# Two token mixers: loops over sequences written out, and the delta rule's second chunk and transposes issued ahead of the second pair's half products

## The chip, the cores and the metric

The kernel runs on one core of one Trainium2 chip. The metric is the device time of the whole program in microseconds (us). A time quoted for a kernel is the median of its runs; a profile is one execution, and its times inside the trace are counted from its first instruction.

## What is computed

Sixteen sequences of 512 tokens with 256 channels go through four layers, each followed by a residual sum and a layer norm, all in float32:

```
x = norm(x + linear_attention(x))     # first mixer: gated, 8 heads
x = norm(x + top2_experts(x))         # 8 experts, capacity limit
x = norm(x + delta_rule(x))           # second mixer: gated delta rule, 4 heads
x = norm(x + composed_mlp(x))         # weights mixed from 32 of 64 primitives
```

The recurrence of the second mixer, for each head, with a state S of 64 by 128:

```
S = S * exp(g_t)
delta = (v_t - k_t S) * b_t
S = S + k_t (x) delta
o_t = q_t S
```

It is worked in chunks of 128 tokens, four to a sequence. A chunk needs the inverse of a unit triangular 128 by 128 matrix for each head. The diagonal blocks of 16 by 16 are inverted on their own, and three rounds of products (levels 4, 5 and 6) merge them to the full inverse.

## The kernel before

There are five parts one after the other: linear attention (the first mixer), routing, the experts, the delta rule (the second mixer) and the closing MLP. In both mixers every engine runs the same order written by hand, one body (`body`) or period (`period`) for each sequence, and engines meet at counting semaphores. The flags of a period say which stages it holds: `front` (projection, convolution and rates of sequence b+1), `here` (the recurrence's first half of sequence b), `past` (second half and output of b-1), `ln` (norms of b+2) and `end` (the last norm of b-2). The first and last periods are written out. The twelve between them, sequences 2 to 13, were a hardware loop of six rounds with two bodies in each:

```
with eng.Fori(0, (B - 4) // 2) as i:
    for u in range(2):
        period(i * 2 + 2 + u, u, here=True, front=True, ln=True, past=True, end=True)
```

Inside the loop the sequence number is a register, and so are the semaphore counts worked out from it.

In the delta rule the order of a period came from 16 slots, eight for each pair of chunks. Slots 5 to 7 and 13 to 15 hold the three levels of a pair. TensorE (PE), for a level and a chunk: `first_half` transposes T into bank UT (L2359) and multiplies (L2363); ScalarE (ACT) copies both results out in `half_level` (U at L2108, Y at L2110); `second_half` multiplies again (L2375, L2377); VectorE (DVE) puts the result into T in `merge` (L1831, or L1826 at level 6, where it is U). UT is one bank, so the next chunk's `first_half` waits for the copy of U.

The diagonal blocks leave and come back by DMA. `key_products` (PE, L2344) gives the products, `key_decays` (DVE, L1809) scales them, `send_blocks` (SyncE's queue) writes them out, GpSimd (POOL) inverts them, and `return_blocks` brings them into T once ACT's `restart` has cleared T. `first_half` of level 4 waits for that landing (`T<-blocks_in`). The factors come from `scan` (DVE, L1800), which `key_decays` needs too.

`chunk(t, part)` is the recurrence itself: part 0 reads the state (PE L2294, L2298; DVE's R at L1843), part 1 is `dl` (PE L2304, copied out by ACT at L2097), part 2 updates state and output (PE L2311, L2315; DVE L1849, L1852). `channels` is PE's twelve transposes of each half of keys and queries of the next sequence (L2275), which ACT's `channel` copies out (L2041). `conv` is DVE's three-step convolution (L1729); it stands between ACT's `tap` (L2007) before it and `conv_silu` (L2012) after it. `reach` (PE, L2332) needs the last of `rates` on DVE (L1771). `norm2` is DVE's L1709 and L1711. In a row, `<-` behind a wait names what ended it.

Of the kernel before, what the change touches and what calls it, by code (L numbers as in the profile page):

```python
# [12 lines left out]
ALU = mybir.AluOpType  # L13
# [4 lines left out]
B, L, D = 16, 512, 256  # L18
NTOK = B * L
DT = D // P  # L20
TT = L // P
# [546 lines left out]
def linear_attention(nc, x_rows, xT_rows, conv_w, wq, wkg, wv, wg, bg, wout, aug_bal, w_gate, x1_rows, logits_out):  # L568

    with ExitStack() as ctx:  # L570
# [87 lines left out]
        with nc.Block() as block:  # L658
# [83 lines left out]
            def _(dve):  # L742
# [190 lines left out]
            def _(act):  # L933
# [105 lines left out]
                with act.Fori(0, (B - 4) // 2) as i:  # L1039
                    for u in range(2):  # L1040
                        body(i * 2 + 2 + u, u, i * 2 + 1 + u, True, i + 2)
# [3 lines left out]
            def _(pe):  # L1045
# [174 lines left out]
                with pe.Fori(0, (B - 4) // 2) as i:  # L1220
                    for u in range(2):
                        body(i * 2 + 2 + u, u, i * 2 + 1 + u, True, i + 2)
# [7 lines left out]

CHUNK_AT = {0: (2, 0), 1: (2, 1), 2: (2, 2), 3: (3, 0), 4: (3, 1), 5: (3, 2),
            9: (0, 0), 10: (0, 1), 11: (0, 2), 12: (1, 0), 13: (1, 1), 14: (1, 2)}
# [121 lines left out]
def delta_rule(nc, x1_rows, slots_out, get_at, weight, ln1_g, ln1_b, rms_w, wq, wk, wv, conv_q, conv_k, conv_v, wa, dt_bias, a_log, wb, wg,  # L1354
               o_norm, wo, ln2_g, ln2_b, w2, b2, x2_rows, hT_rows, blocks_out, blocks_in, x3_wide, fc1, fc2, out_rows):

    with ExitStack() as ctx:
# [115 lines left out]
        def loop(eng, period):  # L1473

            starts(period)
            with eng.Fori(0, (B - 4) // 2) as i:
                for u in range(2):
                    period(i * 2 + 2 + u, u, here=True, front=True, ln=True, past=True, end=True)
            ends(period)

        with nc.Block() as block:
            @block.sync
            def _(sp):
# [81 lines left out]
                loop(sp, period)  # L1565
# [3 lines left out]
            def _(pool):  # L1569
# [88 lines left out]
                loop(pool, period)  # L1658
# [3 lines left out]
            def _(dve):  # L1662
# [128 lines left out]
                def scan(pair, b):  # L1791
                    wait, done = waiter(dve, b)
                    for t in (2 * pair, 2 * pair + 1):
                        i = t % 2
                        wait("aB", t + 1)
                        if t >= 2:
                            wait("kd", t - 1)
                        elif later(b, 0):
                            dve.wait_ge(s["kd"], (b - 1) * TT + t + 3)
                        done("DT", t + 1, v.tensor_tensor_scan(flat(DT_[i][:]), bank[CHUNK[i]][:], flat(id4[:]), 0.0, ALU.mult, ALU.add))  # L1800
# [102 lines left out]
                def period(b, u, here=False, front=False, ln=False, past=False, end=False):  # L1903
                    w = 1 - u
                    for slot in range(2 * (LEVELS + 1)):
                        pair, lv = slot // (LEVELS + 1), slot % (LEVELS + 1) - 1
                        t, part = CHUNK_AT.get(slot, (None, None))
                        if here and lv < 0:
                            key_decays(pair, b)
                        if t is not None and t >= 2 and past:  # L1910
                            chunk(t, part, b - 1, w)
                        if here and lv < 0:
                            query_decays(pair, b)
                        if front and slot == 8:
                            conv(6, b + 1)
                            conv(7, b + 1)
                        if slot == 10 and front:
                            rates(1, b + 1)
                            keys_beta(b + 1)
                        if slot == 11 and past:  # L1920
                            residual(0, b - 1)
                        if t is not None and t < 2 and here:
                            chunk(t, part, b, u)
                        if front and 1 <= slot <= 6:
                            conv(slot - 1, b + 1)
                        if slot == 7 and front:
                            lengths(b + 1)
# [643 lines left out]
```

## Time and profile before

| | us |
|---|---|
| median of 3 runs | 4533.56 |
| lowest and highest run | 4521.59, 4539.57 |
| the profiled execution | 4549.05 |
| its span in the trace | 4547.4 |
| first mixer | 0 to 866 |
| routing, experts | 866 to 2068 |
| delta rule | 2068 to 4072 |
| closing MLP | 4072 to 4547 |

The span is that from the first to the last instruction; 1.65 us of the execution lie outside it. The profiled execution is 15.5 us above the median of the runs. The share of busy time differs much between the parts, so each is read by itself.

### The profile page before, as it was taken

How to read it: one execution, taken by the hardware profiler on the slowest of the kernel's cores; microseconds unless marked ns; L12 is line 12 of the kernel's file. 1: busy time of each engine (PE TensorE's matmuls, PEld its weight loads, DVE VectorE, ACT ScalarE, POOL GpSimd, SP SyncE). 2: the span in 40 equal slices, each digit the busy share in tenths (PEclk: the TensorE clock that was granted, in tenths of full speed). 3: DMA queues.
4: the chain of work that ended last, by engine and by line, in shares of the span. 5: the costliest groups of instructions: out<-in, count | busy, mean ns of one | idle time of the engine just before them, and what ended most of it. 6: DMA issues, size and time to landing. Idle time of an engine off the chain costs nothing.

```text
span 4547.4 us, 72522 instructions
## 1 busy us (share of the span) xinstructions
PE 3962.4 (87%) x23860; PEld 3063.0 (67%) x23860; DVE 2468.9 (54%) x5456; ACT 1990.0 (44%) x4069; POOL 1100.5 (24%) x1686
## 2 busy tenths in 40 slices
PE   6888788598999999994798888888888888879998
PEld 3555555377888888883576666676676677756666
DVE  6888888452222222224577777777777777431111
ACT  5656555111212222122466666666666666432221
POOL 0111111101222222212334444443334343200000
PEclk8888889699999999997799999999999999889999
DMA  1010010254555555552111111111111110011111
GB/s 34 29 42 29 28 40 22 64 147 167 184 183 183 183 183 183 184 181 82 38 35 42 43 43 43 43 43 43 43 42 43 43 43 24 19 58 55 55 55 51
DMA packets 220956, 346.98 MB, mean 76 GB/s; under 512 B 99972, under 2 KB 171908, under 8 KB 202500
## 3 DMA queue, kind: packets, MB, share of 16 engines
q1 hardware_dynamic: 196932, 272.74, 18.9%
q0 software_dynamic: 23760, 71.07, 5.0%
q8 instruction: 123, 2.02, 0.2%
q14 instruction: 141, 1.16, 0.1%
HBM read 276.61 MB, written 68.16 MB: 76 GB/s over the span
## 4 chain that ended last, share of the span: by engine, by line
PE 23%; POOL 8%; issue 8%; DVE 8%; ACT 4%; DMA 2%; SPq 2%; POOLq 0%; DVEq 0%; ACTq 0%
PE gdr_bank L1320 5%; PE gdr_bank L1311 5%; DVE gdr_y L1729 3%; POOL gdr_vblk L1628 2%; PE gdr_bank L2363 2%; POOL gdr_tblk L1626 2%; PE gdr_bank L2375 1%; PE gdr_bank L2240 1%; PE gdr_bank L2359 1%; SPq L1519 1%; POOL gdr_ssq L1616 1%; PE gdr_bank L2408 1%; POOL gdr_orr L1616 1%; POOL gdr_got L1582 1%; POOL gdr_vblk L1623 1%
## 5 line engine op out<-in xcount | busy, mean ns | idle before, releaser
L525 ACT ACTIVATE moe_rel<-moe_fc 128x512 f32<-128x512 f32 x284 | 169.6, 597 | 798.5 <-PE moe_fc L490 798.5
L490 PE MATMUL moe_fc<-moe_xT,moe_win 128*128 128x256 f32 x2272 | 503.8, 380 | 1.5 <-issue 0.8
L501 PE MATMUL moe_o<-moe_wout,moe_hT 128*128 128x256 f32 x2272 | 502.0, 379 | 0.0
L490 PEld LDWEIGHTS moe_fc<-moe_xT,moe_win 128*128 128x128 f32 x2272 | 432.7, 191 | 61.2 <-issue 2.1
L501 PEld LDWEIGHTS moe_o<-moe_wout,moe_hT 128*128 128x128 f32 x2272 | 426.3, 190 | 55.1
L549 DVE TENSOR_TENSOR moe_hT<-moe_rel 128x512 f32<-128x512 f32 x284 | 196.6, 692 | 361.3 <-ACT moe_rel L525 361.3
L1729 DVE SCALAR_TENSOR_TENSOR gdr_y<-gdr_bank,gdr_cw,gdr_y 128x511 f32<-128x511 f32 (+2 forms) x384 | 287.5, 749 | 51.1 <-ACT gdr_y L2007 28.9
L2240 PE MATMUL gdr_bank<-gdr_hT,gdr_wqkv 128*128 128x512 f32 x512 | 263.6, 645 | 31.9 <-ACT gdr_qk L2022 26.8
L558 DVE COPY moe_osb<-moe_o 128x512 f32<-128x512 f32 x71 | 49.1, 692 | 424.9 <-PE moe_o L501 424.9
L2359 PE MATMUL gdr_bank<-gdr_ident,gdr_T 128*128 128x128 f32 x768 | 136.0, 306 | 109.7 <-DMA gdr_T<-blocks_in 95.0
L1311 PE MATMUL gdr_bank<-gdr_hT,gdr_wqkv 128*128 128x512 f32 x512 | 225.4, 599 | 3.5 <-ACT gdr_hT L1329 3.5
L1344 DVE TENSOR_TENSOR gdr_kb<-gdr_bank,gdr_x 128x512 f32<-128x512 f32 x32 | 20.6, 686 | 366.4 <-PE gdr_bank L1320 366.4
L2359 PEld LDWEIGHTS gdr_bank<-gdr_ident,gdr_T 128*128 128x128 f32 x768 | 101.2, 158 | 153.0 <-DMA gdr_T<-blocks_in 73.8
L2363 PE MATMUL gdr_bank<-gdr_T,gdr_nAT 128*128 128x64 f32 (+1 forms) x1536 | 197.6, 278 | 0.0
L2363 PEld LDWEIGHTS gdr_bank<-gdr_T,gdr_nAT 128*128 128x128 f32 (+1 forms) x1536 | 187.3, 198 | 10.9 <-issue 10.9
L2108 ACT COPY gdr_U<-gdr_bank 128x512 f32<-128x512 f32 x192 | 112.4, 585 | 184.4 <-PE gdr_bank L2359 173.9
L2240 PEld LDWEIGHTS gdr_bank<-gdr_hT,gdr_wqkv 128*128 128x128 f32 x512 | 92.7, 199 | 145.5 <-issue 74.4
L1311 PEld LDWEIGHTS gdr_bank<-gdr_hT,gdr_wqkv 128*128 128x128 f32 x512 | 98.3, 192 | 121.2 <-issue 120.4
L446 POOL COPY moe_ix<-slot_token 128x2 uint32 (+1 forms) x71 | 13.0, 183 | 659.9 <-DMA slots_out<-moe_osb 471.8
L1616 POOL TENSOR_TENSOR gdr_rstd<-gdr_var,gdr_mhalf 128x4 f32<-128x4 f32 x64 | 70.9, 1107 | 391.5 <-DVE gdr_var L91 263.5
L450 POOL DMA_INDIRECT moe_xin<-token_rows,moe_ix x142 | 137.3, 967 | 82.8 <-POOL moe_ix L446 58.2
L1333 ACT ACTIVATE gdr_sq<-gdr_bank 128x512 f32<-128x512 f32 x64 | 38.2, 597 | 257.2 <-PE gdr_bank L1311 257.2
(391 smaller groups left out, 8843.1 us busy)
## 6 DMA issues: line engine op xcount, KB each, us to landing
moe_win<-in_moe_w SPq DMA_DIRECT2D x71, 1024.0 KB, 7.9
moe_wout<-in_moe_w SPq DMA_DIRECT2D x71, 1024.0 KB, 5.1
slots_out<-moe_osb POOLq DMA_DIRECT2D x71, 256.0 KB, 7.4
gdr_fz<-mixed_rows SPq DMA_DIRECT2D x18, 512.0 KB, 3.8
gla_xp<-in_xT_rows SPq DMA_DIRECT2D x16, 512.0 KB, 4.7
gla_xres<-in_x_rows SPq DMA_DIRECT2D x16, 512.0 KB, 3.9
token_rows<-gla_x POOLq DMA_DIRECT2D x16, 512.0 KB, 3.4
rt_W<-in_fc_b SPq DMA_DIRECT2D x32, 256.0 KB, 3.4
```

Source lines behind the costliest of these rows:

```text
L450: nc.gpsimd.indirect_dma_start(xin[t][:], None, x_rows, bass.IndirectOffsetOnAxis(ap=ix[:, t:t + 1], axis=0)).then_inc(x_in, 16)
L490: ins = nc.tensor.matmul(fc_ps[j][:, m % 2, :], win[u][:, c, m * P:(m + 1) * P], xT[:, c, :], start=(c == 0), stop=(c == DT - 1))
L501: ins = nc.tensor.matmul(o_ps[u][:, t, :], hT[u][:, k, t * P:(t + 1) * P], wout[u][:, k, :], start=(k == 0), stop=(k == FT - 1))
L525: nc.scalar.activation(rel[:, j, :, :], fc_ps[j][:], ACT.Relu).then_inc(relu_done, 1)
L549: nc.vector.tensor_tensor(hT[u][:, 2 * j:2 * j + 2, :], rel[:, j, :, :], rel[:, j, :, :], ALU.mult).then_inc(h_ready, 1)
L1311: ins = nc.tensor.matmul(fc_ps[m % 4][:], win[:, c, m * P:(m + 1) * P], xT[:, c, :], start=(c == 0), stop=(c == DT - 1))
L1320: ins = nc.tensor.matmul(o_ps[t // 2][:, (t % 2) * D:(t % 2 + 1) * D], hT[k][:, t * P:(t + 1) * P], wout[:, k, :], start=(k == 0), stop=(k ...
L1616: nc.gpsimd.tensor_tensor(out, src, mhalf[:, 0:width], ALU.pow).then_inc(s[name], 1)
L1729: ins = stt(y[:, n % 4, d:L], bank[FRONT[n % 2]][:, 0:L - d], cw[:, n, 3 - d:4 - d], y[:, n % 4, d:L], ALU.mult, ALU.add)
L2240: ins = mm(bank[FRONT[n % 2]][:], wqkv[:, c, n * P:(n + 1) * P], hT[:, c, :], start=(c == 0), stop=(c == DT - 1))
L2359: ins = tp(bank[UT][:, h * P:(h + 1) * P], T[:, i, h, :], ident[:])
L2363: ins = mm(bank[YZ[i]][rows_of(lv), h * HP:(h + 1) * HP].rearrange("p (m n) -> p m n", n=half), nAT[:, i, h, rows_of(lv)], first, start=Tr ...
```

## The change

Both mixers' loops are written out, so that sequence numbers and semaphore counts are constants and no engine branches in them. In the delta rule the table of slots gives way to one written list for each engine. On PE, the second chunk's `dl` and all transposes of the next sequence's second half stand ahead of the second pair's first half product, and `reach` behind part 2 of chunk 0. On DVE, level 4's merges of the first pair stand ahead of `conv(4)`, level 6's merges of the first pair between the two scans, both residuals behind part 2 of chunk 0, `norm2` behind part 0 of chunk 1, and both scans of the next sequence ahead of the bias. On ACT, `restart(1)` stands behind the rates, the copies of `channel` around chunk 1's parts, and `lengths_u`, `keep_keys` and the squares of chunk 0 behind the copies of level 4 or 5. No instruction of the engines' work is added or taken out; SyncE's and GpSimd's lists keep their order.

```
-                with dve.Fori(0, (B - 4) // 2) as i:
-                    for u in range(2):
-                        body(i * 2 + 2 + u, u, i * 2 + 1 + u, True, i + 2)
+                for b in range(2, B - 2):
+                    body(b, b % 2, b - 1, True, b // 2 + 1)
...
-        def loop(eng, period):
+        def loop(period):
...
-            with eng.Fori(0, (B - 4) // 2) as i:
-                for u in range(2):
-                    period(i * 2 + 2 + u, u, here=True, front=True, ln=True, past=True, end=True)
+            for b in range(2, B - 2):
+                period(b, b % 2, here=True, front=True, ln=True, past=True, end=True)
```

VectorE (the written list; conditions on the flags are as before):

```
-                def scan(pair, b):
+                def scan(t, b):
...
+                        chunk(3, 2, b - 1, w)
+                    if here:
+                        merge(4, 0, b)
+                        merge(4, 1, b)
+                    if front:
+                        conv(4, b + 1)
...
+                        scan(2, b)
+                        merge(6, 0, b)
+                        merge(6, 1, b)
+                        scan(3, b)
+                        key_decays(1, b)
+                        query_decays(1, b)
...
+                        rates(1, b + 1)
+                        keys_beta(b + 1)
+                    if here:
+                        chunk(0, 2, b, u)
+                    if past:
+                        residual(0, b - 1)
+                        residual(1, b - 1)
+                    if here:
+                        chunk(1, 0, b, u)
+                    if ln:
+                        norm2(b + 2)
+                    if here:
+                        merge(4, 2, b)
+                        merge(4, 3, b)
```

ScalarE:

```
+                        rates(0, b + 1, w)
+                    if here:
+                        decay_keys(2, b)
+                        decay_keys(3, b)
+                        chunk(0, 1, b, u)
+                    if front:
+                        rates(1, b + 1, w)
+                    if here:
+                        restart(1, b)
+                    if front and here:
+                        act.wait_ge(s["ks"], b * TT + 2)
+                    if front:
+                        channel(0, 0, b + 1, w)
+                        channel(0, 1, b + 1, w)
+                        channel(0, 2, b + 1, w)
+                        channel(1, 0, b + 1, w)
+                    if here:
+                        chunk(1, 0, b, u)
+                        chunk(1, 1, b, u)
+                    if front:
+                        channel(1, 1, b + 1, w)
+                        channel(1, 2, b + 1, w)
+                    if here:
+                        half_level(4, 2, b)
+                        half_level(4, 3, b)
+                    if ln:
+                        lengths_u(b + 2)
```

TensorE:

```
+                    if here:
+                        chunk(0, 1, b, u)
+                        chunk(0, 2, b, u)
...
+                        reach(b + 1)
+                        channels(0, (0, 1), b + 1)
+                    if here:
+                        chunk(1, 0, b, u)
+                    if front:
+                        channels(0, (2,), b + 1)
+                        channels(1, (0,), b + 1)
+                    if here:
+                        chunk(1, 1, b, u)
+                    if front:
+                        channels(1, (1, 2), b + 1)
+                    if here and past:
+                        pe.wait_ge(s["xe"], b * 2)
+                    if here:
+                        first_half(4, 2, b)
+                        first_half(4, 3, b)
+                        second_half(4, 2, b)
+                        second_half(4, 3, b)
+                        first_half(5, 2, b)
+                        chunk(1, 2, b, u)
```

## Rows read from the trace of the kernel before

**Rows 1.** Windows, the delta rule's part: length, busy of each engine, PEclk, DMA share, GB/s.

```profile
2068.00:4072.00 2004.00, 1669.86 (x10696) 1314.17 (x10696) 1364.97 (x3156) 1175.38 (x2789) 727.47 (x1279) 0.91 0.15 42
```

**Rows 2.** Windows of the first mixer's bodies: one written out, two in the loop.

```profile
101.90:149.50 47.60, 40.23 (x377) 26.93 (x377) 43.61 (x85) 30.35 (x45) 7.42 (x3) 0.89 0.11 34
...
543.00:593.40 50.40, 40.57 (x378) 27.17 (x378) 42.22 (x83) 29.57 (x44) 8.02 (x4) 0.86 0.10 32
593.40:641.80 48.40, 40.27 (x379) 26.95 (x378) 42.28 (x83) 29.58 (x44) 8.02 (x4) 0.89 0.10 33
```

**Rows 3.** Waits of VectorE in the first loop: total us, times, longest.

```profile
DVE gla_mu L843 <- issue: 15.3, 5, 3.3
```

**Rows 4.** Windows of the delta rule: periods 8, 9 and 13, the twelve in the loop.

```profile
3096.10:3213.50 117.40, 105.36 (x669) 83.45 (x668) 85.91 (x198) 73.25 (x174) 44.68 (x79) 0.91 0.14 37
3213.50:3328.40 114.90, 99.28 (x671) 78.11 (x670) 85.23 (x198) 73.26 (x174) 45.91 (x79) 0.97 0.17 46
...
3677.70:3790.50 112.80, 98.97 (x669) 78.16 (x668) 85.21 (x198) 73.25 (x174) 36.58 (x67) 0.97 0.12 34
...
2402.20:3790.50 1388.30, 1214.85 (x8017) 960.83 (x8016) 1026.27 (x2376) 879.04 (x2088) 538.75 (x936) 0.95 0.15 41
```

**Rows 5.** Waits of TensorE in the delta rule's loop.

```profile
PE gdr_bank L2359 <- DMA gdr_T<-blocks_in: 61.0, 24, 4.1
...
PE gdr_bank L2294 <- issue: 9.8, 5, 2.6
```

**Rows 6.** Timeline of TensorE, period 9, second half: start, length, instructions, idle before.

```profile
3286.81 0.37 PE L2332 MATMUL gdr_bank<-gdr_sp,gdr_upto 128*128 128x16 f32 x2 [1.43 <-DVE gdr_sp L1771]
...
3297.78 1.11 PE L2359 MATMUL gdr_bank<-gdr_ident,gdr_T 128*128 128x128 f32 x4 [3.99 <-DMA gdr_T<-blocks_in]
...
3300.28 2.02 PE L2304 MATMUL gdr_bank<-gdr_R,gdr_U 128*128 128x128 f32 x8
3302.10 1.06 PE L2359 MATMUL gdr_bank<-gdr_ident,gdr_T 128*128 128x128 f32 x4
...
3305.99 1.04 PE L2275 MATMUL gdr_bank<-gdr_ident,gdr_qk 128*128 128x128 f32 x8
...
3307.77 0.60 PE L2359 MATMUL gdr_bank<-gdr_ident,gdr_T 128*128 128x128 f32 x4
```

**Rows 7.** Timeline of TensorE, period 9, first half.

```profile
3247.73 1.90 PE L2375 MATMUL gdr_bank<-gdr_Y,gdr_U 128*128 128x64 f32 x16
...
3251.39 0.66 PE L2359 MATMUL gdr_bank<-gdr_ident,gdr_T 128*128 128x128 f32 x4
...
3252.99 0.65 PE L2359 MATMUL gdr_bank<-gdr_ident,gdr_T 128*128 128x128 f32 x4
...
3266.37 0.50 PE L2344 MATMUL gdr_bank<-gdr_XT 64*128 64x128 f32 x4 [1.56 <-DVE gdr_U L1826]
```

**Rows 8.** Timeline of VectorE, period 9.

```profile
3248.40 2.31 DVE L1729 SCALAR_TENSOR_TENSOR gdr_y<-gdr_bank,gdr_cw,gdr_y 128x511 f32<-128x511 f32 x3
...
3251.49 0.44 DVE L1831 COPY_PREDICATED gdr_T<-gdr_level,gdr_bank 128x256 f32<-128x256 int32 x1 [0.15 <-DVE gdr_T L1831]
...
3264.55 1.23 DVE L1800 TENSOR_TENSOR_SCAN gdr_DT<-gdr_bank,gdr_id 128x512 f32<-128x512 f32 x1 [0.19 <-DVE gdr_DT L1800]
3265.90 0.95 DVE L1826 COPY gdr_U<-gdr_bank 64x256 f32<-64x256 f32 x2
...
3293.70 1.67 DVE L1709 SCALAR_TENSOR_TENSOR gdr_fz<-gdr_xn,gdr_rstd,gdr_g 128x256 f32<-128x256 f32 x4
...
3296.66 1.13 DVE L1843 SCALAR_TENSOR_TENSOR gdr_R<-gdr_bank,gdr_gbn,gdr_v 128x128 f32<-128x128 f32 x4
```

**Rows 9.** Timeline of ScalarE, period 9, between the two levels.

```profile
3250.81 0.63 ACT L2012 ACTIVATE gdr_y<-gdr_y 128x512 f32<-128x512 f32 x1 [2.24 <-DVE gdr_y L1729]
...
3252.35 0.58 ACT L2108 COPY gdr_U<-gdr_bank 128x512 f32<-128x512 f32 x1
```

**Rows 10.** DMA queues in the delta rule's loop: packets, MB, share of 16 engines.

```profile
q8 instruction: 72, 1.18, 0.4%
```

More of the change, by code:

```diff
@@ L1657, in period @@
                         constants()
-                loop(pool, period)
+                loop(period)
                 fc_gpsimd(pool)
@@ L1980, in _ @@
+                    if past:
+                        bias(1, b - 1)
+                loop(period)
                 fc_vector(dve)
@@ L2216, in _ @@
-                loop(act, period)
+                    if past:
+                        chunk(2, 0, b - 1, w)
+                    if front:
+                        tap(0, b + 1)
+                    if end:
+                        gelu(b - 2)
+                    if front:
+                        tap(1, b + 1)
+                    if past:
+                        chunk(2, 1, b - 1, w)
+                        gate(0, b - 1)
+                    if front:
+                        conv_silu(0, b + 1)
@@ new lines, in period @@
+                    if here:
+                        decay_keys(0, b)
+                        restart(0, b)
+                    if front:
+                        spread_out(0, b + 1)
+                    if past:
+                        gate(1, b - 1)
+                    if front:
+                        conv_silu(1, b + 1)
+                        tap(2, b + 1)
+                    if here:
+                        decay_keys(1, b)
+                    if past:
+                        chunk(3, 0, b - 1, w)
@@ L2503, in _ @@
-                loop(pe, period)
+                    if past and here:
+                        pe.wait_ge(s["DT"], b * TT + 2)
+                    if past:
+                        chunk(2, 0, b - 1, w)
+                    if here and past:
+                        pe.wait_ge(s["Uf"], b * TT)
+                    if here and end:
+                        pe.wait_ge(s["yb"], (b - 1) * 2)
+                    if here:
+                        key_products(0, b, u)
+                    if front:
+                        project(0, b + 1)
+                        project(1, b + 1)
@@ new lines, in period @@
+                    if past:
+                        for c in range(1, DH):
+                            mix_out(c, b - 1)
+                    if here:
+                        chunk(0, 1, b, u)
+                        chunk(0, 2, b, u)
+                    if front and not later(b, -1):
+                        pe.wait_ge(ready, 1)
+                        pe.wait_ge(aprep, 3)
+                    if front:
+                        reach(b + 1)
+                        channels(0, (0, 1), b + 1)
@@ new lines, in period @@
+                    if past:
+                        dense(0, b - 1)
+                    if here:
+                        first_half(6, 3, b)
+                        second_half(6, 2, b)
+                        second_half(6, 3, b)
+                    if ln and front:
+                        pe.wait_ge(s["qkT"], (b + 2) * 6)
+                    if ln:
+                        turn_h(b + 2)
+                    if past:
+                        dense(1, b - 1)
+                loop(period)
```

542 lines of the change are left out of this document (271 added, 271 removed).

## The prediction, made before the run

> **What bounds the kernel now.** I read the windows by part first. The delta rule is the longest of the parts touched: TensorE (PE) is busy for 1669.86 of its 2004 us, VectorE (DVE) for 1364.97 [rows 1]. In the first mixer it is the other way round: a body of the loop takes 48.40 us, in which DVE is busy for 42.28 and PE for 40.27 [rows 2]. So the first mixer is read on DVE and the delta rule on PE.
>
> Next come the waits. In the first loop DVE stands still five times, 15.3 us in all, with nothing that the profile shows to wait for, each time at the first instruction behind the loop's turn [rows 3]. In the delta rule's loop PE does the same five times, 9.8 us in all [rows 5]. Six rounds make five turns, and neither view has such a wait on these lines anywhere else. PE's largest wait is for the diagonal blocks: 61.0 us over 24 landings, two in each of the twelve periods [rows 5].
>
> The timeline of period 9 then shows the order around that landing. PE waits 3.99 us for the second pair's blocks; only after it come chunk 1's `dl`, from 3300.28, and the second half's transposes, from 3305.99 [rows 6].
>
> **The change part by part.** The sum is made against the profiled execution's 4549.05 us and then carried over to the median, 4533.56, which is 15.5 us lower.
>
> *First mixer, the turn of the loop.* A body with the turn in it takes 50.40 us, one without 48.40 [rows 2]: 2.0 us, five times, -10. The gaps themselves add up to 15.3 [rows 3], which is the other bound; the difference of the bodies is what the span pays, so I take 10.
>
> *First mixer, counts as constants.* The body written out before the loop takes 47.60 us against 48.40, though its DVE has more to do, 43.61 against 42.28 [rows 2]. Twelve bodies would give 9.6; but that body also stands at the start, where PE and the first loads are differently placed. I take half, -4.8, with 0 and 9.6 as ends.
>
> *Delta rule, the turn and the counts.* The gaps are 9.8 us [rows 5], and PE is the bound there, so that is the lower end. Period 13, which a written-out period follows, takes 112.80; the twelve took 1388.30, and twelve of 112.80 would be 1353.6, so the upper end is 34.7 [rows 4]. Period 9 less one mean gap of 1.96 is 112.9, like period 13. So the odd periods go there; whether the even ones do isn't shown. I take 20: the gaps, and two fifths of the rest.
>
> A rule of the Trainium skill speaks against both of these terms. The rows show 3.1 us for a gap of DVE and 2.0 for one of PE [rows 3, 5]. The Trainium skill's page "Advanced Engine Details and Errata", section Control Flow Timing, gives a compare-and-branch about 108 ns. By that figure ten turns cost about 1 us, an estimate, where the gaps cost 20, and the sum below would be about 19 smaller. I go by the rows.
>
> *Delta rule, second half.* From 3300.28 to 3302.10 and from 3305.99 to 3307.77 PE works on what now goes ahead of the landing: 1.82 + 1.78 = 3.60 us a period [rows 6]. It can go there only if its inputs are ready. R of chunk 1 is made at 3296.66, behind `norm2`, which starts at 3293.70; the new order puts R first, so it is there some 2.9 us earlier [rows 8], about 3294.9. With ACT's copies between the transposes I find PE through with the moved work at about 3297.0, ahead of the landing at 3297.78 [rows 6]. What hides it is that wait. `reach` and its 1.43 us of waiting [rows 6] also move, behind chunk 0's part 2, and so does `restart(1)`: costed at nothing, because both lie ahead of the same landing; without that cover 1.4 more would be gained.
>
> Two things are taken off. `key_decays` of the second pair now stands behind a scan of 1.23 us [rows 8] that used to be done before the copies; DVE waits for PE there, and I put 0.5 on the landing. And `first_half`, `first_half`, `second_half`, `second_half`, `first_half` now follow each other with nothing between: a copy of U is 0.58 [rows 9], a merge 0.44 [rows 8], each mostly under the other chunk's products; I put 0.9 for the waits. That leaves 2.2 us, for the 15 periods that have both stages: -33. Ends: 0, if the blocks come later by all that was won; and 5.7, if PE's lower clock in that stretch goes too. Four transposes took 1.11 us behind the landing and 0.66 at 3251.39 [rows 6, 7]; of the 9.99 us from 3297.78 to 3307.77, 6.39 aren't moved, and at 0.66 for 1.11 they would take 3.8, so 3.60 + 2.6 - 0.5.
>
> *Delta rule, first half.* Here the change adds a wait. `conv(4)` starts at 3248.40 [rows 8]; now the two merges of level 4 stand ahead of it, and the second can't start before PE's `second_half` ends at 3247.73 + 1.90 = 3249.63 [rows 7]. With a merge of 0.44 behind that, `conv(4)` starts near 3250.3, 1.9 later. Behind it on ACT are `conv_silu`, `tap` and only then level 5's copy of U, which starts 1.64 us after the convolution's end [rows 8, 9]. PE's next transposes, at 3252.99 [rows 7], need that copy at once: they go to 3254.9. What the earlier merge gives PE is next to nothing here, as its first transposes of level 5 began at 3251.39, as soon as `project` was through [rows 7]. In return the copies of level 6 go between the scans: PE's wait of 1.56 at 3266.37 was for these, which came at 3265.90 behind a second scan begun at 3264.55 [rows 7, 8]; up to 1.35 is saved. The one wait moves into the other: 1.9 less 1.35 and what is left of the 1.56. I take 0, with -1.35 and +1.9 a period as ends, -20 and +29.
>
> *Sum.* -10 - 4.8 - 20 - 33 + 0 = -68. Against the profiled execution 4481; against the median 4465, which I predict. All ends on the good side would give 15.3 + 9.6 + 34.7 + 86 + 20 = 166 less, all on the bad one 10 + 9.8 less and 29 more, about +9.
>
> **Rivals.** Times are from the median.
>
> 1. *The late convolution isn't made up.* DVE waits for ACT's squares before the scans, so the 1.35 is not found: +29, 4494. For it: PE's copy of U was just in time, with no slack [rows 7, 9]. Against: the 1.56 of idle time is there to swallow it. Chance 0.18.
>
> 2. *The lower clock behind the landing goes too,* because the wait before it shrinks from 4 us to about 1. Half of the 2.6 and the 0.9 of new waits come back: 2.2 more a period, -33, 4432. Against it: PE still waits for copies between the moved pieces. Chance 0.11.
>
> 3. *Slower: the new wait costs PE its clock.* Periods 8 and 9 run the same instructions, yet PE is busy for 105.36 us in the one, at a mean granted clock of 0.91, and for 99.28 in the other at 0.97 [rows 4]: 6.1 us. If the 1.9 us of waiting at level 5 brings that to twelve more periods, it is +73, and with rival 1's 29 the time is 4567. It decides from about eleven such periods on. Against it: period 9 has its waits without it. Chance 0.07.
>
> 4. *Written-out code runs dry.* If each of 24 written-out bodies had one gap of 2.0, in place of ten gaps now, 28 would be lost and 20 not won: 4513. Against: inside the loop instructions are already streamed, 72 packets of 1.18 MB on one queue [rows 10], and the gaps are at turns alone [rows 3, 5]. Chance 0.05.
>
> 5. *The gap isn't the turn's* and stays at the head of a body: 19.8 less is won, 4485. This is what the page's figure for a branch would give. Chance 0.05.
>
> The forecast has 0.54.
>
> **How the numbers follow.** About 0.5% is what a measurement of this kernel can tell from no change: 4511 to 4556. The forecast, rivals 1, 2 and 5 end below that, but for some of their spread; rival 4 on its edge; rival 3 above. That gives faster 0.85, same 0.09, slower 0.06. The range reaches from beyond rival 2, with the first half's gain, 4405, to 4515, which takes in rivals 1, 5 and 4; rival 3 and the far ends stay out.
>
> **What would show it.** After the change neither "issue" wait is left on L843's and L2294's successors. A body of the first mixer takes 47.6 to 48.4 throughout. PE's wait for the blocks falls from 4 us to about 1 for the second pair and stays as it is for the first. A new wait of about 1.9 us stands before the second chunk's transposes of level 5, and the wait of the second pair's key products is gone or small. A period takes about 110 to 111. I am wrong if the blocks land later than their chain of today, if `restart(1)` becomes what their return waits for, or if periods at a clock of 0.91 become the rule.

## The result, and the profile after

| | us |
|---|---|
| before, median of 4 runs beside it | 4529.94 |
| after, median of 4 runs | 4478.48 (4467.55 to 4483.57) |
| ratio, 95% interval | 0.9876 (0.9844 to 0.9907) |
| predicted | 4465, range 4405 to 4515 |
| profiled execution after, its span | 4473.65, 4472.0 |

The kernel became 56 us faster by the ratio (0.0124 of 4534); the sum had said 68. The runs below show that the total came near by luck: the delta rule's loop and its second half gave more than their terms, and its first half, put at nothing, cost 40 to 54 us.

First the windows of the changed kernel: a body of the first mixer, then periods 11 and 12, then the fourteen periods 1 to 14 in one window, each with length, busy time of PE, PEld, DVE, ACT and POOL, PEclk, DMA share and GB/s.

```profile
392.30:440.10 47.80, 40.36 (x385) 27.11 (x381) 42.17 (x83) 29.61 (x45) 8.03 (x4) 0.89 0.11 35
...
3390.40:3499.30 108.90, 97.51 (x669) 76.66 (x668) 85.25 (x198) 73.32 (x174) 44.02 (x78) 0.98 0.15 43
3499.30:3611.00 111.70, 99.37 (x669) 77.36 (x668) 85.39 (x198) 73.30 (x174) 46.45 (x80) 0.97 0.16 45
...
2273.34:3831.82 1558.48, 1390.75 (x9346) 1093.93 (x9345) 1180.13 (x2722) 1021.03 (x2424) 613.11 (x1079) 0.97 0.15 41
```

TensorE's waits in the same fourteen periods of the kernel before (total us, times, longest):

```profile
PE gdr_bank L2359 <- DMA gdr_T<-blocks_in: 69.0, 28, 4.1
PE gdr_bank L2332 <- DVE gdr_sp L1771: 22.5, 14, 2.0
...
PE gdr_bank L2344 <- DVE gdr_U L1826: 18.9, 13, 1.6
...
PE gdr_bank L2311 <- ACT gdr_dl L2097: 9.3, 25, 0.5
PE gdr_bank L2359 <- ACT gdr_U L2108: 6.2, 15, 0.7
PE gdr_bank L2359 <- DVE gdr_T L1831: 5.2, 8, 1.0
```

Their window:

```profile
2293.18:3899.97 1606.79, 1411.23 (x9345) 1116.84 (x9344) 1181.78 (x2722) 1020.13 (x2424) 615.18 (x1078) 0.95 0.15 40
```

And TensorE's waits of the changed kernel:

```profile
PE gdr_bank L2428 <- DMA gdr_T<-blocks_in: 34.6, 22, 2.5
PE gdr_bank L2428 <- ACT gdr_U L2126: 29.9, 18, 2.1
PE gdr_bank L2373 <- DVE gdr_R L1835: 19.1, 14, 1.4
PE gdr_bank L2380 <- ACT gdr_dl L2115: 18.4, 27, 1.3
...
PE gdr_bank L2428 <- DVE gdr_T L1823: 13.3, 14, 1.0
...
PE gdr_bank L2413 <- DVE gdr_U L1818: 3.2, 14, 0.6
```

A window's length less PE's busy time is its idle time: 195.6 us before, 167.7 after. So of the 48.3 us by which the fourteen periods became shorter, 27.8 are waiting and 20.5 are the same products run faster, at a mean clock of 0.97 for 0.95. Half of the blocks' wait is gone, and so are `reach`'s wait (22.5) and most of the key products' (18.9 to 3.2). But 23.7 us of new waiting for U have come, 19.1 for R, 8.1 for T (13.3 for 5.2) and 9.1 for `dl`. The "issue" waits of [rows 3, 5] have no successor on L843 or L2363.

Where the clock came back is seen in the ten us behind the second pair's landing, in period 9 before and in period 11 after:

```profile
3297.78:3307.78 10.00, 9.76 (x61) 9.52 (x62) 1.98 (x9) 4.52 (x13) 0.00 (x0) 0.70 0.00 0
...
3475.00:3485.00 10.00, 10.00 (x92) 9.67 (x92) 5.35 (x14) 7.13 (x19) 0.02 (x1) 1.00 0.06 11
```

It is so in all fourteen periods: a mean granted clock of 0.58 to 0.83 in these ten us before, 0.97 to 1.00 after. Between the first pair's landing and the second's, in turn, the mean fell from 0.96 to 0.94.

### The profile page after: what moved, and what is told of

It is laid out like the page before. It is cut to its first block, busy times and chain, and to the rows that moved or that the text cites. A ratio compares the mean times of both kernels' runs of the same rounds, so it can differ in the third digit from the quotient of the medians.

```text
span 4472.0 us, 69167 instructions
## 1 busy us (share of the span) xinstructions
PE 3932.8 (88%) x23860; PEld 3035.3 (68%) x23860; DVE 2466.4 (55%) x5456; ACT 1991.2 (45%) x4069; POOL 1098.8 (25%) x1686
## 3 DMA queue, kind: packets, MB, share of 16 engines
q1 hardware_dynamic: 196932, 272.74, 19.1%
## 4 chain that ended last, share of the span: by engine, by line
PE 26%; DVE 8%; POOL 6%; DMA 4%; SPq 3%; issue 3%; ACT 2%; DVEq 0%; ACTq 0%; POOLq 0%
PE gdr_bank L1314 5%; PE gdr_bank L1305 5%; POOL gdr_vblk L1621 2%; PE gdr_bank L2432 2%; POOL gdr_tblk L1619 2%; PE gdr_bank L2444 2%; PE gdr_bank L2428 2%; SPq L1500 2%; DVE gdr_y L1722 2%; SPq L1512 2%; PE gdr_bank L2392 1%; PE gdr_bank L2477 1%; DMA gdr_wblk<-blocks_out 1%; PE gdr_bank L2309 1%; DMA blocks_in<-gdr_vblk 1%
## 5 line engine op out<-in xcount | busy, mean ns | idle before, releaser
L2428 PE MATMUL gdr_bank<-gdr_ident,gdr_T 128*128 128x128 f32 x768 | 126.1, 290 | 100.4 <-DMA gdr_T<-blocks_in 53.6
L2432 PE MATMUL gdr_bank<-gdr_T,gdr_nAT 128*128 128x64 f32 (+1 forms) x1536 | 185.4, 267 | 0.0
L2432 PEld LDWEIGHTS gdr_bank<-gdr_T,gdr_nAT 128*128 128x128 f32 (+1 forms) x1536 | 173.7, 186 | 10.7 <-issue 10.7
```

The source lines that it names most:

```text
L2428: ins = tp(bank[UT][:, h * P:(h + 1) * P], T[:, i, h, :], ident[:])
L2432: ins = mm(bank[YZ[i]][rows_of(lv), h * HP:(h + 1) * HP].rearrange("p (m n) -> p m n", n=half), nAT[:, i, h, rows_of(lv)], first, start=Tr ...
```

## The experiments

Ratios are to the kernel before, run on the same chip beside each call (medians 4533.46, 4539.16 and 4538.75 us). A difference of two ratios is turned into us with the median before, 4534.

**The loops.** The first run writes out the first mixer's loops, on three engines:

```
-                with dve.Fori(0, (B - 4) // 2) as i:
-                    for u in range(2):
-                        body(i * 2 + 2 + u, u, i * 2 + 1 + u, True, i + 2)
+                for b in range(2, B - 2):
+                    body(b, b % 2, b - 1, True, b // 2 + 1)
```

> The kernel before with the first mixer's three loops written out and nothing else changed. Theory: the loop's turn and its register counts cost 50.40 us with and 48.40 us without a turn, where the written-out body now takes 47.77 us; five turns of 2.0 us and fourteen bodies that are some 0.6 us shorter give -18 us, so about 4515 us (ratio 0.996), a first mixer of about 847 us in the trace and no issue wait on L843. Rival one: only the turns go, -10 us, 4524 us. Rival two: the gap belongs to the head of the body and not to the turn, so it is also seen in written-out code, and the time stays at 4533 us.

Measured: 4513.29 us, 0.9962 (0.9949 to 0.9976), -17 us. In its trace the first mixer ends 19.6 us sooner. Five turns were 10.8 of that (the distances of the bodies' last logits, 50.4 to 50.7 with a turn, 48.35 without), and most of the rest is bodies of 47.7 to 47.9 us from end to end.

The second run writes out the delta rule's loop too, in its old order:

```
-            with eng.Fori(0, (B - 4) // 2) as i:
-                for u in range(2):
-                    period(i * 2 + 2 + u, u, here=True, front=True, ln=True, past=True, end=True)
+            for b in range(2, B - 2):
+                period(b, b % 2, here=True, front=True, ln=True, past=True, end=True)
```

> The kernel before with both mixers' loops written out and the delta rule in its old order. Theory: -18 us in the first mixer and -20 us in the delta rule (between -10 and -35), 4495 us or a ratio of about 0.9915; the periods lie near 113 us, with PE's 4 us wait for the second pair's blocks still there. Rival one: in the delta rule the written-out loop is all of the gain and the new order none, so this is as fast as the changed kernel, 4478 us (0.988). Rival two: other waits of the period take up the turns' gaps, the delta rule gains nothing from it, and the time is 4515 us.

Measured: 4479.71 us, 0.9883 (0.9869 to 0.9897). That is rival one: as fast as the whole change. The delta rule's loop is worth 36 us (0.9962 less 0.9883), and the new order, with all that it moves, nothing. Where the 36 come from is seen by TensorE's waits over the fourteen periods, first in the run with the loop:

```profile
PE gdr_bank L2356 <- DMA gdr_T<-blocks_in: 76.1, 28, 4.5
...
PE gdr_bank L2341 <- DVE gdr_U L1823: 20.3, 14, 1.6
...
PE gdr_bank L2291 <- issue: 8.6, 5, 2.2
```

And by window:

```profile
2270.93:3869.83 1598.90, 1400.18 (x9345) 1109.91 (x9344) 1179.94 (x2722) 1020.88 (x2424) 618.55 (x1078) 0.96 0.14 40
```

Then without:

```profile
PE gdr_bank L2355 <- DMA gdr_T<-blocks_in: 72.7, 28, 4.2
...
PE gdr_bank L2340 <- DVE gdr_U L1822: 15.7, 14, 1.3
```

And by window:

```profile
2266.36:3834.54 1568.18, 1397.11 (x9346) 1113.05 (x9345) 1180.51 (x2722) 1020.21 (x2424) 619.47 (x1078) 0.96 0.15 41
```

Idle time falls by 27.6 us (198.7 to 171.1), and only 8.6 of it is the gap at the turn. The other 19 lie in smaller falls of most other waits: 4.6 at the key products, 3.4 at the blocks, and 0.4 to 3 each at the copies and merges; `reach`'s wait doesn't fall.

The third run is the counterpart: the new order with both loops kept (the changed kernel with the two edits above taken back).

> The changed kernel with both mixers' loops kept as loops, so that only the delta rule's new order is left. Theory as predicted: the new order is worth 33 us, 4500 us (ratio 0.993). Rival one: it is worth what the change has left over after the loops, some 17 us, because the new wait of 2.08 us for the copy of U and the half clock behind it (a first half of 56 us in place of 52.3 us) give back half: 4517 us (0.996). Rival two: the new order is worth nothing by itself, 4533 us.

Measured: 4535.61 us, 1.0008 (0.9996 to 1.0019): rival two. The new order alone is worth nothing with the loops either. (Its trace isn't read here: it is of the lowest of thirteen runs, 4499.15 us.)

The last of this group (the twelfth run) asks what a turn costs, with four bodies a round in place of two, in both mixers:

```
-            with eng.Fori(0, (B - 4) // 2) as i:
-                for u in range(2):
-                    period(i * 2 + 2 + u, u, here=True, front=True, ln=True, past=True, end=True)
+            with eng.Fori(0, (B - 4) // 4) as i:
+                for u in range(4):
+                    period(i * 4 + 2 + u, u % 2, here=True, front=True, ln=True, past=True, end=True)
```

> The kernel before with both mixers' loops as three rounds of four bodies in place of six of two: two turns in place of five in each, and the sequence numbers still in registers. Both loops written out gave -54 us. Theory, the prediction's split: a turn costs about 2.0 us in either loop and the rest belongs to counts as constants, so six turns fewer give -12 us, 4522 us (ratio 0.9974). Rival: nearly all of the 54 us belongs to the ten turns and what follows from them (the order of waits and the clock behind a gap), so three fifths of it go: -32 us, 4501 us (0.993).

Measured: 4513.32 us, 0.9947 (0.9933 to 0.9961), -24 us for six turns, between the theory and the rival. The gaps that are left, two in each mixer, are 3.15 us each on DVE and 1.45 on PE; so a turn costs about 4.0 us of the whole, more than its gap on the engine that bounds the stage. That is a mean of two kinds: by this trace the first mixer ends only 3.9 us sooner (one of its two turns takes 5.1 us), so most of the 24 came in the delta rule. What is left to the constants, 53 less ten turns of 4.0, is some 13 us; the interval of this run (18 to 30 us) makes that anything from 2 to 24, so the total alone hardly tells it from nothing.

The trace does. With fewer turns and the numbers still in registers, a body of the first mixer without a turn takes 48.2 to 48.7 us, as before, and not 47.7 to 47.9, and PE's wait for the key products stands as before (18.9) and not as without the loop (15.7):

```profile
PE gdr_bank L2344 <- DVE gdr_U L1826: 18.6, 14, 1.6
```

So these shorter handoffs belong to the constants and not to the turns.

**The new order.** Why it is worth nothing is seen on TensorE, in periods 11 and 12, whose first parts are alike. By timeline, from the first landing's level on:

```profile
3425.95 1.94 PE L2309 MATMUL gdr_bank<-gdr_hT,gdr_wqkv 128*128 128x512 f32 x4
...
3431.24 0.63 PE L2428 MATMUL gdr_bank<-gdr_ident,gdr_T 128*128 128x128 f32 x4 [2.08 <-ACT gdr_U L2126]
...
3432.99 1.90 PE L2444 MATMUL gdr_bank<-gdr_Y,gdr_U 128*128 128x64 f32 x16
3434.73 1.94 PE L2309 MATMUL gdr_bank<-gdr_hT,gdr_wqkv 128*128 128x512 f32 x4
...
3540.56 0.63 PE L2428 MATMUL gdr_bank<-gdr_ident,gdr_T 128*128 128x128 f32 x4 [2.08 <-ACT gdr_U L2126]
...
3542.30 3.48 PE L2444 MATMUL gdr_bank<-gdr_Y,gdr_U 128*128 128x64 f32 x16
3545.57 3.72 PE L2309 MATMUL gdr_bank<-gdr_hT,gdr_wqkv 128*128 128x512 f32 x4
```

The wait of 2.08 us is there in each of the fourteen periods. Behind it, in period 12, the same products take 3.48 and 3.72 us in place of 1.90 and 1.94: half clock. That is so in four of the fourteen periods. What makes the wait is on the other two engines, in period 11, first VectorE:

```profile
3423.81 0.69 DVE L1844 TENSOR_TENSOR gdr_o<-gdr_bank,gdr_QSe 128x512 f32<-128x512 f32 x1
...
3425.36 0.43 DVE L1823 COPY_PREDICATED gdr_T<-gdr_level,gdr_bank 128x256 f32<-128x256 int32 x1
...
3426.26 0.43 DVE L1823 COPY_PREDICATED gdr_T<-gdr_level,gdr_bank 128x256 f32<-128x256 int32 x1
3426.72 2.32 DVE L1722 SCALAR_TENSOR_TENSOR gdr_y<-gdr_bank,gdr_cw,gdr_y 128x511 f32<-128x511 f32 x3
```

Then ScalarE:

```profile
3429.13 0.63 ACT L2037 ACTIVATE gdr_y<-gdr_y 128x512 f32<-128x512 f32 x1 [4.07 <-DVE gdr_y L1722]
3429.79 0.69 ACT L2032 ACTIVATE gdr_y<-gdr_bank,gdr_cw 128x512 f32<-128x512 f32 x1
3430.51 0.59 ACT L2126 COPY gdr_U<-gdr_bank 128x512 f32<-128x512 f32 x1
```

`conv(4)` starts at 3426.72, behind both merges, though DVE was free from 3424.5; ACT stands 4.07 us for it, and the copy of U that PE needs is third in ACT's queue. The fourth run puts `conv(4)` back ahead of the merges:

```
+                    if front:
+                        conv(4, b + 1)
                     if here:
                         merge(4, 0, b)
                         merge(4, 1, b)
-                    if front:
-                        conv(4, b + 1)
```

> The changed kernel with VectorE's conv(4) back ahead of the two merges of level 4 of the first pair; nothing else. Theory: PE's wait of 2.08 us for the copy of U at level 5 is made by this convolution and falls to about 0.4 us, 1.7 us in each of 15 periods or -25 us against the changed kernel's 4478 us: 4453 us (ratio 0.983); should the half clock behind this wait be its consequence, the periods with a first half of 56 us become rare and up to 3.8 us more goes in ten of them, 4415 us (0.974). Rival one: the wait moves to another place of the first half (the merges now end later, so PE waits for T instead, or the key products wait for the scans as in the kernel before, 1.5 us): 4475 us (0.988).

Measured: 4429.29 us, 0.9788 (0.9764 to 0.9811). TensorE's waits over the fourteen periods:

```profile
PE gdr_bank L2428 <- DMA gdr_T<-blocks_in: 41.6, 24, 3.8
...
PE gdr_bank L2428 <- ACT gdr_U L2126: 4.2, 16, 0.3
```

And by window:

```profile
2266.65:3792.12 1525.47, 1378.18 (x9346) 1085.59 (x9345) 1180.96 (x2722) 1021.00 (x2424) 613.16 (x1079) 0.98 0.15 42
```

The wait for U is gone (29.9 to 4.2), 7.0 of it come back at the blocks, and PE's busy time falls by 12.6 besides. This one edit is worth 40 us by the ratios (about 22 to 58 by their intervals) and 49 by the medians, more than the theory's 25 for the wait and less than its 63 with all clocks had back.

The reverse (the sixth run): the old order, both loops written out, with the merges of level 4 ahead of `conv(4)` and nothing else.

```
+                        if here and slot == 5:
+                            merge(lv, 2 * pair, b)
+                            merge(lv, 2 * pair + 1, b)
                         if front and 1 <= slot <= 6:
                             conv(slot - 1, b + 1)
...
-                        if here and lv >= BASE:
+                        if here and lv >= BASE and slot != 5:
```

> Both loops written out in the old order (4480 us), with one edit: the two merges of level 4 of the first pair ahead of conv(4). Theory: this edit alone is what cost the change its gain: the wait of 2.08 us for the copy of U appears at level 5, 1.8 us more than the 0.27 us of the old order, and the clock halves behind it in some periods, together +50 us, 4530 us (ratio 0.999). Rival one: only the wait itself, +27 us, 4507 us (0.994). Rival two: the old order swallows it in the wait of 1.07 us for the key products, because the convolutions that end later are not what those wait for: +11 us, 4491 us (0.991).

Measured: 4540.07 us, 1.0003 (0.9990 to 1.0016), which is +54 against the same kernel without the edit (0.9883), as the theory had it. TensorE's waits:

```profile
PE gdr_bank L2358 <- DMA gdr_T<-blocks_in: 83.7, 28, 5.5
PE gdr_bank L2358 <- ACT gdr_U L2107: 29.1, 14, 2.1
```

And by window:

```profile
2272.08:3898.02 1625.94, 1426.99 (x9345) 1133.55 (x9344) 1181.24 (x2722) 1020.98 (x2424) 618.84 (x1078) 0.94 0.14 40
```

Idle time is 27.9 us more than in the second run (199.0 to 171.1), busy time 29.9 more for the same instructions, at a mean clock of 0.94 for 0.96. So the wait is paid once as waiting and once more as clock: behind it the products take 3.5 us for 1.90 in ten of the fourteen periods.

Is it the late convolution, or the copy's place behind it? In the seventh run DVE stays as changed here; ACT's first copies of level 5 go ahead of `conv_silu(4)`:

```
                     if front:
                         spread_out(3, b + 1)
+                    if here:
+                        half_level(5, 0, b)
+                    if front:
                         conv_silu(4, b + 1)
                         tap(5, b + 1)
                     if here:
-                        half_level(5, 0, b)
                         half_level(5, 1, b)
```

> The changed kernel, VectorE's order untouched, with ScalarE's first copies of level 5 (half_level(5, 0)) ahead of conv_silu(4) and tap(5). Theory: the wait of 2.08 us is made by the copy of U standing behind conv_silu(4), which waits for conv(4); so taking the copy out of that queue does the same as moving the convolution: the wait falls to some 0.3 us and the time to about 4430 us (ratio 0.978). Rival: the late convolution itself is what costs the time, through conv_silu(4), to_tokens(4) and the next projection, and a new wait of 1 to 2 us stands at those transposes: 4465 to 4478 us (0.985 to 0.988).

Measured: 4449.51 us, 0.9807 (0.9786 to 0.9828). PE's wait for U falls to 11.5 us in all, with 0.8 as its longest:

```profile
PE gdr_bank L2430 <- ACT gdr_U L2126: 11.5, 17, 0.8
```

Most of the gain comes (31 of 40 us by the ratios; the other 9 lie within the intervals). So the copy's place in ACT's queue is the main mechanism; what the late convolution costs by itself is at most the rest.

The scans (the fifth run): `scan(3)` ahead of level 6's merges again, on top of the fourth run.

```
                         scan(2, b)
+                        scan(3, b)
                         merge(6, 0, b)
                         merge(6, 1, b)
-                        scan(3, b)
```

> The changed kernel with conv(4) ahead of the merges (4429 us) and, on top of it, both scans of the second pair ahead of the two merges of level 6 again. Theory, the prediction's 1.35 us a period: PE's wait for the second pair's key products, now 0.20 us, goes back to the 1.07 us that it has in the old order with both loops written out, or more: 0.9 to 1.35 us in 15 periods, +13 to +20, 4442 to 4449 us (ratio 0.980 to 0.982). Rival: the splitting is worth nothing, because key_decays behind the second scan sets when the blocks land, and it is as late either way: 4429 us (0.979).

Measured: 4445.33 us, 0.9786 (0.9761 to 0.9810), beside the fourth run's 0.9788. By the ratios that is the rival's nothing, but the two intervals leave some 15 us either way, so the theory's 13 isn't excluded. The key products' wait does go back, from 0.20 to some 1.1 us in most periods, 15.8 in all; the blocks' wait falls from 41.6 to 36.3 for it. In TensorE's waits:

```profile
PE gdr_bank L2428 <- DMA gdr_T<-blocks_in: 36.3, 22, 2.6
...
PE gdr_bank L2413 <- DVE gdr_U L1818: 15.8, 14, 1.3
```

By window:

```profile
2270.87:3805.87 1535.00, 1380.85 (x9345) 1088.59 (x9344) 1182.01 (x2722) 1021.06 (x2424) 613.32 (x1079) 0.97 0.15 42
```

In these fourteen periods the run is 9.5 us longer than the fourth, 6.9 of it waiting (154.2 for 147.3): by the traces the split is worth about half of what the theory had, by the totals nothing that can be told.

This run against the second (0.9883) is also the new second half all but alone: -44 us, of it in the fourteen periods 16.9 of waiting and 16.3 of busy time.

**Wait or clock.** In the ninth run four products of 128 by 512 with unread results go into the wait of the changed kernel:

```
                         first_half(5, 0, b)
+                    if here and past:
+                        fill(SIDE, 4)     # mm(bank[SIDE][:], ident[:], wqkv[:, 0, 0:512])
+                    if here:
                         first_half(5, 1, b)
```

> The changed kernel, with four products of 128 by 512 whose results nobody reads added on PE in each period between the two first products of level 5, so that PE works (4 times 0.46 us, as the projection's products take) through most of the wait of 2.08 us. The lateness of the copy stays. Theory: the lower clock behind this wait follows from PE's standing still, so with PE busy the first halves of 56 us become halves of 52.3 us in some nine periods, -30 us, 4449 us (ratio 0.981), although PE has 28 us more to do. Rival: the clock falls by itself or for the landing wait ahead of it; then nothing is gained and the products cost up to a few tenths of a us in each period: 4478 to 4490 us (0.988 to 0.991).

Measured: 4489.14 us, 0.9886 (0.9868 to 0.9904), in the rival's range. But the products were sized wrong: one is two instructions of 0.46 us, and the four took 3.65 us, for 2.08 of waiting, by the timeline of period 9:

```profile
3202.95 3.65 PE L2483 MATMUL gdr_bank<-gdr_wqkv,gdr_ident 128*128 128x512 f32 x8
...
3208.16 1.90 PE L2444 MATMUL gdr_bank<-gdr_Y,gdr_U 128*128 128x64 f32 x16
```

That is 1.6 us too much in each period, +22. The products behind the wait kept 1.90 us, and in all fourteen periods, where four had 3.5 without the filling; that much of the theory holds. But half clock behind the landings stayed, and the blocks' wait grew from 34.6 to 46.3 us. So the run tells that nothing was won in time, and not what a filling of the right size would give.

**A better version.** The waits that were left asked for three more moves on top of the fourth run (the eighth run): on PE `chunk(3, 2)` ahead of the first pair's first product and `to_tokens(3)` between its two; on DVE `last_norm` behind `chunk(3, 2)`, `conv(4)` and level 4's merges, and `chunk(1, 2)` ahead of `decay`, with `values_beta(0)` behind level 5's merges.

```
+                    if past:
+                        chunk(3, 2, b - 1, w)
                     if here:
                         first_half(4, 0, b)
-                    if past:
-                        chunk(3, 2, b - 1, w)
+                    if front:
+                        to_tokens(3, b + 1)
                     if here:
                         first_half(4, 1, b)
...
+                    if past:
+                        chunk(3, 2, b - 1, w)
+                    if front:
+                        conv(4, b + 1)
+                    if here:
+                        merge(4, 0, b)
+                        merge(4, 1, b)
                     if end:
                         last_norm(b - 2)
...
+                    if here:
+                        chunk(1, 2, b, u)
...
                         decay(b + 1, w)
-                        values_beta(0, b + 1, w)
...
-                        chunk(1, 2, b, u)
                         merge(5, 2, b)
                         merge(5, 3, b)
                     if front:
+                        values_beta(0, b + 1, w)
```

> The changed kernel with conv(4) ahead of the merges and three more moves: on PE chunk(3, 2) ahead of the first pair's first product and to_tokens(3) between its two products, so that the wait of 1.7 to 2.5 us for the first landing is filled; on VectorE last_norm behind the merges of level 4, and chunk(1, 2) ahead of decay and values_beta, so that the wait of 0.96 us before the transposes of level 6 goes. Theory: 1.2 and 0.96 us a period, -30 us against 4429: 4400 us (ratio 0.971). Rival: the landings take it back, as the second pair's blocks land when they did and PE waits for them instead: 4425 us (0.976).

Measured: 4407.00 us, 0.9705 (0.9685 to 0.9726), the fastest without useless work: 38 us below the fourth run by the ratios, 22 by the medians, as the theory had it (4400). PE's wait for T at level 6 is gone, and the blocks' falls from 41.6 to 25.6. The trace is of the slowest of its five runs, 4415.79 us. In it period 4 takes 104.9 us at full clock, period 7 takes 114.4, and most of the difference is in the second half:

```profile
2587.80:2692.70 104.90, 96.15 (x671) 75.30 (x670) 85.47 (x198) 73.31 (x174) 47.06 (x80) 1.00 0.16 47
2907.10:3021.50 114.40, 103.90 (x669) 83.00 (x668) 85.37 (x198) 73.32 (x174) 47.29 (x81) 0.93 0.16 46
```

By timeline, period 7's second pair:

```profile
2992.16 0.63 PE L2429 MATMUL gdr_bank<-gdr_ident,gdr_T 128*128 128x128 f32 x4 [2.00 <-DMA gdr_T<-blocks_in]
...
2996.37 3.62 PE L2445 MATMUL gdr_bank<-gdr_Y,gdr_U 128*128 128x64 f32 x16
```

Products with unread results, five a period, were added ahead of this landing (the tenth run), and in the eleventh run two at the first landing as well; the five:

```
+                    if here and past:
+                        fill(YZ[0], 3)
                     if here:
                         chunk(1, 1, b, u)
                     if front:
                         channels(1, (1, 2), b + 1)
+                    if here and past:
+                        fill(YZ[0], 2)
```

> The kernel with the first landing's wait filled (4407 us), with products whose results nobody reads added on PE in each period: three ahead of chunk(1, 1), where PE waits 1.37 us for R, and two ahead of the second pair's first product, where it waits 0.9 to 2.3 us for the blocks. Theory: the long periods of that kernel (112.0, 114.4, 113.3 and 110.8 us, where most take 105) have their half clock behind these waits, so all periods take 105 us, -26 us, 4381 us (ratio 0.965). Rival: the clock isn't had back by this and the products delay the landing's users by some 0.5 us a period: 4407 to 4415 us (0.971 to 0.973).

Measured: 4399.42 us, 0.9695 (0.9681 to 0.9708), between the theory and the rival.

> As the run with the products at R and at the second landing, and two more such products ahead of the first pair's first product, where that kernel still waits 0 to 2.6 us for the first landing. Theory: one period in fifteen had its half clock there, so some -4 us more: 4377 us (ratio 0.964). Rival: where the blocks have landed already the products cost 0.9 us a period, +10 us against the run without them.

Measured: 4409.20 us, 0.9711 (0.9696 to 0.9727), 10 us more than the run before, as the rival had it. The window of the former's fourteen periods:

```profile
2266.14:3754.84 1488.70, 1398.45 (x9486) 1078.58 (x9485) 1179.93 (x2722) 1020.22 (x2424) 628.88 (x1081) 1.00 0.15 43
```

The clock is 1.00 in every period, as the theory had it, and all take 104 to 107 us. The 140 instructions more take 64.7 us; without them PE's own work is 1333.8 us, for 1376.5 in the run without them. The time of the two is the same within the intervals (0.9695 and 0.9705). Here too the products took twice what was reckoned: three of them, some 2.7 us at 0.91 each, stand in R's wait of 1.37, which fits the 1.4 us by which a period is longer than the best ones without them (106.4 for 105).

## Why the prediction was right, and where it was not

| term | predicted | measured |
|---|---|---|
| first mixer, turn and counts | -14.8 | -17 |
| delta rule, turn and counts | -20 (-10 to -35) | -36 |
| delta rule, second half | -33 (0 to -86) | -44 |
| delta rule, first half | 0 (-20 to +29) | +40 to +54 |
| sum | -68 | -56 |

The measured terms add up to -57 to -43.

*First mixer.* Right in both parts, by the trace: 10.8 us for the turns and 7 to 9 for the rest. The body of 47.6 us of [rows 2] was the better guide, and half of it was too careful.

*Delta rule's loop.* The mechanism holds, the size is the range's far end, which came from period 13 of [rows 4]. "Two fifths of the rest" was the choice that failed: nearly all of the rest went too. By its waits, most of what idle time fell by is not the gap but many shorter handoffs.

Of the rule weighed in the prediction the trace now says more. With the loops gone the gaps are gone and none has come elsewhere, so they were the turns' (rival 5 falls) and not the code's length (rival 4 falls). The Trainium skill's page "Runtime: NRT & Kernel Launch", section Instruction fetch mechanics, says that a taken branch to a target outside what is held waits for a fetch; the gaps of 3.1 and 2.0 us [rows 3, 5] agree with that, and not with the 108 ns that the prediction weighed. The trace of the kernel before shows instructions being loaded there, though not for which engine: in each of DVE's five gaps one packet of instructions starts 1.1 us after the gap's beginning, and in each of PE's five one starts 0.9 to 1.7 us after it. In DVE's gap from 543.54 to 546.49:

```profile
q14 instruction: 1, 0.01, 0.7%
```

*Second half.* Right in its place: the moved work went ahead of the landing, whose wait fell to between nothing and 1.0 us. The 1.43 of `reach`, costed at nothing, was had. Not foreseen were PE's waits for R (1.37, in each period) and for T at level 6 (0.96). These cost more than `reach` gave: 19.1 and 12.3 us in the fifth run, for the 21.7 of the second. "The new order puts R first" was a misreading: both residuals and their statistics stand ahead of R on DVE. The second landing's lower clock went nearly whole, as rival 2 had it: in the ten us behind that landing it is 0.66 to 0.83 in every period of the second run, 0.96 to 1.00 in all but one of the fifth. About half of the 33 us that the trace shows is busy time.

*First half.* This is the step that failed, and it is the sentence "The one wait moves into the other". The wait of 1.9 was forecast with its place and cause and came as 2.08. But the 1.35 set against it was had only in part. With the loops written out that wait is already 1.1 us, for 1.56 before; the split takes some 0.9 of it, and by the fifth run's trace about 0.4 of that goes again at the blocks. So rival 1 was nearly right there. And the wait was priced at its own length, where it also costs clock: in the sixth run 29.9 us of busy time beside 27.9 of waiting. That was the mechanism of rival 3, held for 0.07. Its "period 9 has its waits without it" was true of single periods and no evidence for all of them.

So the total was near by luck. The changed order gains some 44 us in one place and loses 40 to 54 in another, where the forecast had 33 and nothing, and the loop's 16 us more than its term made up for about half of what was missing.

## What to carry to other kernels

Before an instruction is put behind a short one on an engine, follow the next engine's queue: a convolution some 2 us later on DVE became a wait of PE of 2.08 because a copy stood third behind it on ACT. A hardware loop's price isn't its gap alone: most handoffs inside were a little shorter when sequence numbers and counts were constants. Judge an order by parts: here one edit taken back was worth 40 us, and the whole change 56.

## What the runs showed of the hardware

A wait of about 2 us can be followed by products at half of TensorE's clock (3.48 for 1.90 us, 1.2 GHz for 2.4) and in the next period not be. Behind the wait of 2.08 us for U it was so in four of fourteen periods of the changed kernel and in ten of the sixth run; with the wait filled, in none. Which of the two comes in a period, no run here settles. The Trainium skill's page "TensorE: Matmul & The Clock Gate", section HAM oscillation, tells of products that start at the low clock after a wait for a DMA and advises an order of the loop that keeps the engine warm. The trace agrees (0.70 behind the landing of period 9 before), also for a wait for a copy by ScalarE. With PE kept busy through its longest waits the granted clock was 1.00 in all fourteen periods of the tenth and the eleventh run, but the useless products, longer than the waits, gave that back. A product of 128 by 512 in float32 is two instructions of 0.46 us at full clock, 0.91 in all (eight took 3.65).
